# First batch's attention alone, its experts with the second batch's attention between, and expert weights in 512 KB pieces

## What is computed

```python
q, k, v = split_heads(x @ Wq.T), split_heads(x @ Wk.T), split_heads(x @ Wv.T)
attn = softmax(where(causal, q @ k.T * 8 ** -0.5, -inf))
x = layernorm(x + (attn @ v) @ Wo.T)
scores = sigmoid(x @ router_w.T); sfc = scores + e_bias
# group score = sum of the two best of 8; keep 4 of 8 groups, then the best 8 experts
coef[t, e] = 2.5 * scores[t, e] / sum(scores of the chosen)
h = silu(einsum(x, Wg)) * einsum(x, Wu) * coef
moe = einsum(h, Wd); shared = silu(x @ SWg) * (x @ SWu) @ SWd
x = layernorm(x + moe + shared)
```

## Time and profile before

| | us |
|---|---|
| median of three runs | 1035.29 |
| lowest, highest | 1033.92, 1036.24 |
| profiled execution | 1035.23 |
| its span | 1033.2 |

### The profile page before, as it was taken

One profiled execution on the slowest core, in us unless ns is written; L12 is line 12 of the kernel. 1 busy time (PEld: TensorE's weight loads), 2 busy tenths in 40 slices (PEclk: granted clock), 3 DMA queues, 4 the chain that ended last, 5 costly groups with the idle time before them and its releaser, 6 DMA issues.

```text
span 1033.2 us, 15722 instructions
## 1 busy us (share of the span) xinstructions
PE 936.0 (91%) x4800; PEld 564.4 (55%) x4800; DVE 810.7 (78%) x2435; ACT 462.3 (45%) x882; POOL 626.7 (61%) x668
## 2 busy tenths in 40 slices
PE   2687699999999899999999899999999999988996
PEld 1233356665566556665566556665566556655653
DVE  5765767798978997799977997798977986587554
ACT  2354345444444444445444444444444545433332
POOL 2432137665676556675676556675676667765775
PEclk7588689999999999999999999999999999999998
DMA  8441153332533253323533253322533232322331
GB/s 297 144 142 49 35 177 109 116 106 103 173 106 116 94 177 110 116 84 124 173 106 116 88 175 118 116 76 103 195 91 116 95 100 83 112 75 84 102 123 51
DMA packets 63075, 120.75 MB, mean 117 GB/s; under 512 B 7056, under 2 KB 34576, under 8 KB 62608
## 3 DMA queue, kind: packets, MB, share of 16 engines
q1 hardware_dynamic: 62992, 119.76, 36.0%
HBM read 97.32 MB, written 22.02 MB: 116 GB/s over the span
## 4 chain that ended last, share of the span: by engine, by line
PE 63%; DVE 27%; issue 4%; DMA 3%; POOL 2%; ACT 1%; SPq 0%; POOLq 0%; DVEq 0%
PE acc L594 8%; DVE max_out L890 7%; PE ob L541 7%; PE sm L511 5%; PE pu L472 5%; PE pg L472 5%; PE st L529 5%; PE pg L474 4%; PE pg L473 4%; PE pu L474 4%; PE pu L473 4%; DVE hid L963 4%; DVE hid L954 3%; PE acc L584 3%; PE acc L586 2%
## 5 line engine op out<-in xcount | busy, mean ns | idle before, releaser
L706 POOL TENSOR_TENSOR hid<-hid,coef_b 128x512 f32<-128x512 f32 x256 | 332.2, 1298 | 197.1 <-DVE hid L963 182.8
L655 ACT ACTIVATE hid<-pg 128x512 f32<-128x512 f32 x264 | 157.7, 597 | 359.9 <-PE pg L474 358.6
L890 DVE CUSTOM_DVE_ANT_0 max_out<-sm,causal_sb 128x128 bf16<-128x128 f32 (+3 forms) x512 | 235.6, 482 | 90.7 <-PE sm L511 89.3
L954 DVE SCALAR_TENSOR_TENSOR hid<-hid,pg 128x512 f32<-128x512 f32 x264 | 180.2, 682 | 86.9 <-ACT hid L655 86.9
L710 POOL TENSOR_TENSOR hid_lo<-hid,hid_hi 128x512 fp32r<-128x512 f32 x128 | 164.2, 1283 | 71.3 <-ACT hid_hi L662 70.0
L627 ACT ACTIVATE probs<-st 128x512 f32<-128x512 f32 (+1 forms) x384 | 187.1, 526 | 20.4 <-PE st L529 18.5
L963 DVE TENSOR_TENSOR hid<-hid,pu 128x512 f32<-128x512 f32 x256 | 174.6, 682 | 10.9 <-PE pu L474 6.2
L511 PE MATMUL sm<-k_stack,q_stack 72*128 72x128 bf16 (+3 forms) x512 | 140.9, 323 | 32.3 <-DMA k_stack<-k_rows_dram 16.5
L692 POOL TENSOR_SCALAR_AFFINE_SELECT probs<-probs 128x256 f32<-128x256 f32 x256 | 102.8, 426 | 75.4 <-ACT probs L627 74.9
L472 PE MATMUL pg<-x_hi,wg_hi 128*128 128x512 f32 x256 | 139.6, 545 | 9.8 <-DVE hid L954 9.7
L472 PE MATMUL pu<-x_hi,wu_hi 128*128 128x512 f32 x256 | 125.0, 488 | 15.7 <-DVE hid L963 15.6
(11 more groups left out here) (129 smaller groups left out, 1213.1 us busy)
## 6 DMA issues: line engine op xcount, KB each, us to landing
coef_b<-coef_dram SPq DMA_DIRECT2D x128, 512.0 KB, 3.9
q_rows_dram<-qk_parts SPq DMA_DIRECT2D x24, 384.0 KB, 3.3
k_rows_dram<-qk_parts SPq DMA_DIRECT2D x24, 384.0 KB, 3.7
q_stack<-q_rows_dram SPq DMA_DIRECT2D x64, 144.0 KB
k_stack<-k_rows_dram SPq DMA_DIRECT2D x64, 144.0 KB
xT_sb<-in_xT SPq DMA_DIRECT2D x8, 256.0 KB, 3.9
y<-in_x SPq DMA_DIRECT2D x8, 256.0 KB, 4.4
out<-out_sb SPq DMA_DIRECT2D x8, 256.0 KB, 2.4
```

What stands on the lines that cost most here:

```text
L706: pool.tensor_tensor(hid[:, i % 3, :], hid[:, i % 3, :], coef_b[:, half % 2, j, :], ALU.mult)\
L890: last = dve.tensor_tensor_reduce(out=max_out[:, seg.nth(BANK_SM, task) % 2, col:col + wide], in0=sm_of(seg, task)[:, col:col + wide], in1 ...
L954: dve.scalar_tensor_tensor(hid[:, i % 3, :], hid[:, i % 3, :], 1.0, pg[:, :], ALU.add, ALU.mult).then_inc(a_done, 1)
```

## The change

All batches now come from one `order`. Batch 0's attention has its old places (`FIRST_ARGS`, routing steps slightly denser). Its experts begin right behind x1T, at place 31.5 of the old scale (`MOE_AT`); the early units are drawn out by up to 2.5 units (`MOE_LATE`). Batch 1 and all later ones have `STEADY` places, drawn together by a factor of 0.77 up to place 40 (`HEAD_RATE`, `HEAD_END`). The weights come in eleven pieces of at most 512 KB: the shared one into `hid`, ten in turn into the halves of `coef_b`, evenly spaced, all but the shared one cut by GpSimd. `wd_sb` is loaded behind the last piece, and TensorE waits for it at d0.2.

```diff
-SPLIT_BY_DVE = 3
-CHUNKS = 9
+SPLIT_BY_DVE = 1
+CHUNKS = 11
...
+FIRST_ARGS = (5.5, 10.5, 1.05, -3.25, (2.6, 4.3, 8.05, 10.9, 0.55), 27.75, 0.06)
+MOE_AT = 31.5
+HEAD_END, HEAD_RATE = 40.0, 0.77
+MOE_LATE = 2.5
+WEIGHT_LOADS = tuple(4.4 + 1.7 * i for i in range(CHUNKS))
+WEIGHT_SPLITS = tuple(at + 2.0 for at in WEIGHT_LOADS)
...
+def order():
+    out = [(at - MOE_AT, kind, 0, i) for at, kind, i in FIRST]
+    out += [(at - MOE_AT, "wld", 0, j) for j, at in enumerate(WEIGHT_LOADS)]
+    out += [(at - MOE_AT, "chunk", 0, j) for j, at in enumerate(WEIGHT_SPLITS)]
+    for n in range(1, B):
         for at, kind, i in STEADY:
+            at += n * UNITS
+            out.append((at - (1 - HEAD_RATE) * min(at - HEAD_END, 0), kind, n, i))
+    for n in range(B):
+        for at, kind, i in moe_places():
+            late = MOE_LATE * (1 - at / UNITS) if n == 0 and i != SHARED and at < UNITS else 0
+            out.append((n * UNITS + at + late, kind, n, i))
...
+                        if i == CHUNKS - 1:
+                            sp.dma_start(wd_sb[:, :], Wd[:, PAIRS // 2 * D:]).then_inc(wd_in, 16)
...
+                            if (n, i) == (0, 2):
+                                pe.wait_ge(wd_in, 16)
```

46 lines of the change are left out of this document (12 added, 34 removed).

## The result

The changed kernel takes 1074.19 us (median of four runs, 1073.74 to 1074.84) where before takes 1034.61 us (median of four runs as well): a ratio of 1.038, 95% interval 1.036 to 1.040. The direction of the prediction was right and its size was not: +39.6 us where +5.8 was predicted, outside the range of 1031 to 1049. The profiled execution has a span of 1073.1 us (before 1033.2).

What follows compares the result with a forecast made beforehand. TensorE was taken to bound the middle stages, waits the opening. Terms: -3.3 us up to batch 0's x1T copy, -3.2 to its first down product, +12.3 to batch 2's experts: 1035.2 + 5.8 = 1041.0 us, range 1031 to 1049.

Steps and rivals of the forecast that it cites:

- the factor that sized this prediction: Between batch 0's first down product and batch 2's first expert product: 0.9 on 13.7 us of pushed TensorE work, giving +12.3 us.

## What to carry to other kernels

A stretch in which the bounding engine waits for a chain is a place to put work, not to take it from: work that was free there costs its full time and new waits where it goes (22.4 us for 13.7), while adding ready products to the gap, with nothing else touched, won about 1 us. Before comparing two executions by one or two us, compare their granted clocks: one fall was worth 1.5 us here, and the factor that sized this prediction held one. When a change rewrites an order, compare the two lists task by task at every mark where one stage hands over to the next, for what moved inside a stretch and for how ties fall, and not only the sets ahead of a few marks. Before moving an elementwise step to an engine that is free, look at what the other engine does at that moment.

## What the runs showed of the hardware

While GpSimd subtracts a piece of 1024 columns (2.35 us), a VectorE cast of 0.42 us takes 2.41 and a subtraction of 16 columns, 0.17 us, takes 2.24: the short step ends within 0.3 us of GpSimd's, so its price is what is left of the other engine's instruction and not its own. Ten such pieces cost VectorE 7.3 us of busy time. Yet most of VectorE's steps in the neighbourhood, such as the row maxima read from PSUM (0.68 us at 59.55), kept their length; which steps are held was not tested one by one.

TensorE's granted clock also falls within stages in which it is busy nearly all the time. In before it was busy for 2.43 of 4 us, then ran at 0.50 of full from 243 to 246 us, busy throughout, with products of 0.63 us instead of 0.40. The same list without the fall took 1.5 us less (99.1 instead of 100.6).
